# A state-space layer and a mixture-of-experts transformer layer on one core: PSUM banks and products regrouped in the second phase

## The reference, cut to what matters

```python
h = rmsnorm(x, ln1_w)
q, k, v = split(h @ wqkv.T)                # 16 query heads, 4 key/value heads, 8 features each, rope on q and k
scores = q @ k.T * scale                   # causal
attn = softmax(scores) @ v
x = x + attn @ wo.T
h = rmsnorm(x, ln2_w)
logits = h @ gate_w.T                      # 8 experts
topw, topi = top_k(softmax(logits), 2)     # two experts a token, weights normalised
for e in range(8):
    g = silu(h @ w1[e].T) * (h @ w3[e].T)  # 256 wide
    out = out + (g @ w2[e].T) * wfull[:, e:e + 1]
return x + out
```

## Time and profile before

| | us |
|---|---|
| median of 3 runs | 2104.83 (2100.11 to 2111.2) |
| the profiled execution | 2109.42 |
| its span | 2107.6 |
| mean granted clock of PE | 0.802 of full speed |

### The profile page before, as it was taken

How to read it: one execution, slowest core, us unless ns; L and a number is a source line. 1 busy time by engine, 2 the same in 40 slices (tenths; PEclk the granted TensorE clock), 3 DMA queues, 4 the chain that set the end, 5 groups by cost and what they waited for, 6 DMA issues and landing times.

```text
span 2107.6 us, 29882 instructions
## 1 busy us (share of the span) xinstructions
PE 1465.6 (70%) x8536; PEld 1038.4 (49%) x8536; DVE 1600.7 (76%) x2570; ACT 1138.5 (54%) x1901; POOL 1377.4 (65%) x1224
## 2 busy tenths in 40 slices
PE   3767676676666677666527777788787887888663
PEld 1544454454445455444413444565656565656553
DVE  3999999999999999999614656566767666765443
ACT  4655565655556565556112775656565656565410
POOL 1776777777777777677542775648676767767633
PEclk8887777887777888777555988889888888888877
DMA  4210212220121212022021012424252433442453
GB/s 157 86 66 32 85 80 101 80 100 10 74 97 80 101 80 79 22 81 96 5 60 34 28 43 73 125 75 131 88 151 91 141 97 106 129 128 84 136 175 104
DMA packets 113890, 185.00 MB, mean 88 GB/s; under 512 B 9856, under 2 KB 86656, under 8 KB 109440
## 3 DMA queue, kind: packets, MB, share of 16 engines
q1 hardware_dynamic: 109664, 175.14, 24.5%
q0 software_dynamic: 4096, 8.40, 1.4%
HBM read 153.03 MB, written 25.89 MB: 85 GB/s over the span
## 4 chain that ended last, share of the span: by engine, by line
PE 18%; DVE 11%; POOL 7%; issue 6%; DMA 5%; ACT 2%; SPq 1%; another core or an unknown queue 0%; POOLq 0%; DVEq 0%; ACTq 0%
PE og L1306 3%; DVE mx L1678 3%; POOL pp L2033 3%; PE ms L1252 2%; POOL xs_scratch L2042 2%; DMA xg<-xs_scratch 2%; PE pbk L1375 2%; PE po L1385 2%; PE scores L1287 1%; PE ms L1250 1%; DVE rec L1707 1%; PE pa L1368 1%; DMA xs_scratch<-h2n,posi 1%; DVE h L1640 1%; PE m L1347 1%
## 5 line engine op out<-in xcount | busy, mean ns | idle before, releaser
L731 POOL TENSOR_TENSOR hc<-hb,cb 128x512 f32<-128x512 f32 x512 | 654.5, 1297 | 248.2 <-DVE hb L610 218.4
L610 DVE TENSOR_TENSOR_SCAN hb<-da,dbu 128x512 f32<-128x512 f32 x512 | 598.9, 1200 | 5.6 <-DVE stats L635 4.0
L499 ACT ACTIVATE da<-dt,a_neg 128x512 f32<-128x512 f32 x512 | 351.9, 717 | 353.8 <-DVE hb L610 302.6
L2033 POOL TENSOR_TENSOR pp<-pt,pp 128x512 f16<-128x512 f32 x320 | 377.6, 1184 | 230.1 <-ACT pt L1534 225.4
L1678 DVE TENSOR_REDUCE mx<-ms 128x1 f32<-128x384 f32 (+3 forms) x352 | 224.8, 639 | 298.4 <-PE ms L1252 296.4
L331 PE MATMUL yp<-ident,hc 128*128 128x128 f32 x2048 | 358.6, 317 | 66.0 <-POOL hc L731 65.6
L331 PEld LDWEIGHTS yp<-ident,hc 128*128 128x128 f32 x2048 | 297.8, 165 | 175.4 <-POOL hc L731 94.2
L1533 ACT ACTIVATE pp<-scores,lift 128x512 f16<-128x512 f32 x320 | 219.0, 684 | 205.7 <-PE scores L1287 203.2
L603 DVE TENSOR_TENSOR dbu<-dtu,bp 128x512 f32<-128x512 f32 x512 | 323.2, 675 | 3.0 <-PE bp L319 1.6
L319 PE MATMUL bp<-st,sel 96*128 96x512 bf16 x256 | 116.5, 456 | 155.3 <-DVE dbu L603 152.9
L1534 ACT ACTIVATE pt<-scores,lift 128x512 f32<-128x512 f32 x320 | 218.8, 684 | 0.0
(11 more groups left out here) (194 smaller groups left out, 2436.0 us busy)
## 6 DMA issues: line engine op xcount, KB each, us to landing
cb<-c_scratch SPq DMA_DIRECT2D x16, 3072.0 KB, 11.9
wt<-ffn_w_e SPq DMA_DIRECT2D x120, 384.0 KB, 3.8
cb<-c_scratch SPq DMA_DIRECT2D x16, 1024.0 KB, 4.6
q<-q_scratch SPq DMA_DIRECT2D x96, 96.0 KB
xg<-xs_scratch SPq DMA_DIRECT2D x8, 960.0 KB, 5.7
ys_scratch<-ysb SPq DMA_DIRECT2D x24, 256.0 KB, 2.3
q_scratch<-qp SPq DMA_DIRECT2D x24, 128.0 KB
k<-k_scratch SPq DMA_DIRECT2D x32, 72.0 KB
```

The costliest lines, as they stand in the source:

```text
L499: nc.scalar.activation(da[:, s % NDA, :], dt[:, d, h, :], ACT.Exp, scale=a_neg[:, d, h, n:n + 1]).then_inc(da_done, 1)
L610: nc.vector.tensor_tensor_scan(hb[:, s % NHB, :], da[:, s % NDA, :], dbu[:, s % 2, :], 0.0, ALU.mult, ALU.add).then_inc(scan_done, 1)
L731: nc.gpsimd.tensor_tensor(hc[:, s % NHC, :], hb[:, s % NHB, :], cb[:, d, s // 2, :], ALU.mult).then_inc(hc_done, 1)
L2033: nc.gpsimd.tensor_tensor(pp[:, (ST_TILES * b + t) % NPR, 1, 0:width], pt[:, (ST_TILES * b + t) % NPR, 0:width], pp[:, (ST_TILES * b + t) ...
```

## The change

- The bank `pbk` is gone; `ms` has two banks, used in turn, and `pe_max(t)` waits for the reduction before the last one. The experts' rows, gate and up products all use `pa`: `pe_a` of f = 0 waits for `xt`, `pe_bm` for `ga` of its own half, `pe_a` of f = 1 for `g` of the first half.
- The down products have slots of their own (`down_at`: f = 0 nine and f = 1 thirteen slots behind 10q), and the copy out of `po` comes in slot 10q + 14 (`out_at`). For q = 3 these are slots 39, 3 and 4.
- For the masks of several heads there is one product with the mask repeated, over a strided output, in `pe_max` and `pe_st`.
- The count is in bf16 (`prefix` converted once by POOL, `chosen` written as bf16) and has five products instead of eleven: those of earlier blocks and the sum are one product a block, with `chosen` repeated. It moves from slot 25 to 27.
- `dve_gate`'s steps get slots by the table `GATE_AT` (20 to 32); the three steps of `wsum` and `wn` move from the end (24 to 26) to 12 to 14, so all later steps have numbers higher by three. The scatters move to slots 31 to 38.

```diff
+GATE_AT = (20, 20, 21, 21, 21, 22, 22, 23, 23, 24, 25, 25, 26, 26, 26, 28, 28, 28, 29, 29, 29, 30, 30, 31, 31, 32, 32)
...
+def down_at(b, t):
+
+    for q in range(NG):
+        for f, at in ((0, 10 * q + 9), (1, 10 * q + 13)):
+            found = b - 2 - at // ST_TILES
+            if t == at % ST_TILES and valid(found):
+                return found, q, f
+    return None
...
+def out_at(b, t):
+
+    for q in range(NG):
+        at = 10 * q + 14
+        found = b - 2 - at // ST_TILES
+        if t == at % ST_TILES and valid(found):
+            return found, q
+    return None
...
-        chosen = sb("chosen", [P, TC, NE])
+        chosen = sb("chosen", [P, TC, NE], BF16)
...
-        pbk = pb("pbk", [P, SEQ])
         po = pb("po", [P, SEQ])
         m0 = pb("m0", [P, SEQ])
-        ms = pb("ms", [P, SEQ])
+        ms = pb("ms", [P, 2, SEQ])
...
-            pe.wait_ge(max_done, count(max_done, b, t))
+            pe.wait_ge(max_done, count(max_done, b, t - 1))
             width = (c + 1) * P
+            heads = ms[:, t % 2, 0:n * width].rearrange("p (n k) -> p n k", n=n)
+            nc.tensor.matmul(heads[:, :, c * P:width], identb[:, :], mask[:, 0, :].unsqueeze(1).to_broadcast([P, n, P]),
+                             start=True, stop=False, skip_group_check=True)
             for i in range(n):
-                at = i * width
-                nc.tensor.matmul(ms[:, at + c * P:at + width], identb[:, :], mask[:, 0, :],
-                                 start=(i == 0), stop=False, skip_group_check=True)
-                last = nc.tensor.matmul(ms[:, at:at + width],
-                                        q9[0:PART_ROWS, h0_ + i, c * P:(c + 1) * P],
+                last = nc.tensor.matmul(heads[:, i, :], q9[0:PART_ROWS, h0_ + i, c * P:(c + 1) * P],
                                         k9[0:PART_ROWS, (h0_ + i) // 4, 0:width],
                                         start=False, stop=True, skip_group_check=True)
             last.then_inc(max_ready, 1)
...
-            for i, (h, kc, at) in enumerate(pieces(t)):
-                nc.tensor.matmul(sp_[:, t % 2, at:at + P], identb[:, :], mask[:, 1, :],
-                                 start=(i == 0), stop=False, skip_group_check=True)
+            ps = pieces(t)
+            blocks = sp_[:, t % 2, :].rearrange("p (n k) -> p n k", k=P)[:, 0:ps[-1][2] // P + 1:max(ps[-1][2] // P, 1)]
+            nc.tensor.matmul(blocks, identb[:, :], mask[:, 1, :].unsqueeze(1).to_broadcast([P, len(ps), P]),
+                             start=True, stop=False, skip_group_check=True)
+            for h, kc, at in ps:
...
-            for c in range(TC - 1):
-                for later in range(c + 1, TC):
-                    nc.tensor.matmul(m0[:, later * NE:(later + 1) * NE], prefix[:, 1, :], chosen[:, c, :],
-                                     start=False, stop=False, skip_group_check=True)
             for c in range(TC):
-                last = nc.tensor.matmul(m0[:, TC * NE:(TC + 1) * NE], prefix[:, 1, :], chosen[:, c, :],
+                later = m0[:, (c + 1) * NE:(TC + 1) * NE].rearrange("p (n e) -> p n e", e=NE)
+                last = nc.tensor.matmul(later, prefix[:, 1, :], chosen[:, c, :].unsqueeze(1).to_broadcast([P, TC - c, NE]),
                                         start=False, stop=(c == TC - 1), skip_group_check=True)
             last.then_inc(cnt_ready, 1)
...
-                last = nc.tensor.transpose(pbk[:, i * P:(i + 1) * P], xg[:, j, :], ident[:, :])
+                last = nc.tensor.transpose(pa[:, i * P:(i + 1) * P], xg[:, j, :], ident[:, :])
             last.then_inc(xg_ready, 1)
 
         def pe_a(pe, b, q, f):
-            n = NF * q + f
             if f == 0:
                 pe.wait_ge(w_loaded[q], count(w_loaded[q], b, 16 * len(tiles(q))))
-            pe.wait_ge(ga_done, count(ga_done, b, n))
-            pe.wait_ge(xt_done, count(xt_done, b, q + 1))
+                pe.wait_ge(xt_done, count(xt_done, b, q + 1))
+            else:
+                pe.wait_ge(g_done, count(g_done, b, NF * q + 1))
             for i, j in enumerate(tiles(q)):
                 last = nc.tensor.matmul(pa[:, i * P:(i + 1) * P], wt[:, j % NWT, f * P:(f + 1) * P], xt[:, j * P:(j + 1) * P],
                                         start=True, stop=True)
             last.then_inc(a_ready, 1)
 
         def pe_bm(pe, b, q, f):
-            pe.wait_ge(g_done, count(g_done, b, NF * q + f))
+            pe.wait_ge(ga_done, count(ga_done, b, NF * q + f + 1))
             for i, j in enumerate(tiles(q)):
-                last = nc.tensor.matmul(pbk[:, i * P:(i + 1) * P], wt[:, j % NWT, FF + f * P:FF + (f + 1) * P],
+                last = nc.tensor.matmul(pa[:, i * P:(i + 1) * P], wt[:, j % NWT, FF + f * P:FF + (f + 1) * P],
                                         xt[:, j * P:(j + 1) * P], start=True, stop=True)
             last.then_inc(b_ready, 1)
...
             q, j = k // 5, k % 5
             if j == 0:
-                if q > 0:
-                    pe_down(pe, b, q - 1, 1)
-                elif valid(b - 1):
-                    pe_down(pe, b - 1, NG - 1, 1)
                 pe_xg(pe, b, q)
             if j == 1:
                 pe_a(pe, b, q, 0)
@@ -1403,7 +1418,6 @@
                 pe_a(pe, b, q, 1)
             if j == 4:
                 pe_bm(pe, b, q, 1)
-                pe_down(pe, b, q, 0)
...
-                    if t == 25:
+                    if t == 27:
+                        if post == 0:
+                            pe.wait_ge(casts, 3)
                         pe_count(pe, post)
...
                 if step := moe_at(b, t):
                     pe_moe(pe, *step)
-                elif t == 2 and valid(end):
-                    pe_down(pe, end, NG - 1, 1)
+                if step := down_at(b, t):
+                    pe_down(pe, *step)
...
-                elif t == 2 and valid(end):
-                    act_y(act, end, NG - 1)
+                if step := out_at(b, t):
+                    act_y(act, *step)
...
-                    if t == 20:
-                        dve_gate(dve, post, 0)
-                    if 21 <= t <= 33:
-                        dve_gate(dve, post, 2 * (t - 21) + 1)
-                        dve_gate(dve, post, 2 * (t - 21) + 2)
+                    for k in range(GATE_STEPS):
+                        if t == GATE_AT[k]:
+                            dve_gate(dve, post, k)
...
-                    if 30 <= t < 30 + TC * TOP:
-                        pool_scatter(pool, post, t - 30)
+                    if 31 <= t < 31 + TC * TOP:
+                        pool_scatter(pool, post, t - 31)
...
+                if b == 1:
+                    pool.wait_ge(rest_loaded, n_rest)
+                    nc.gpsimd.tensor_copy(prefix[:, :, :], prefix32[:, :, :]).then_inc(casts, 1)
```

More of the change, by code:

```diff
@@ L865, in ffn_phase @@
         tri = sb("tri", [P, NE, NE])
-        prefix = sb("prefix", [P, 2, P])
+        prefix32 = sb("prefix32", [P, 2, P])
+        prefix = sb("prefix", [P, 2, P], BF16)
         pick = sb("pick", [P, TOP])
@@ L1037, in ffn_phase @@
                          (mask32, "mask"))
-        rest_weights = ((wo, "wo"), (gate, "gate"), (tri, "tri"), (prefix, "prefix"), (pick, "pick"), (full, "full"),
+        rest_weights = ((wo, "wo"), (gate, "gate"), (tri, "tri"), (prefix32, "prefix"), (pick, "pick"), (full, "full"),
                         (tile_no, "tile_no"))
@@ L1123, in sp_w @@
         def sp_w(sp, b, q):
-            chosen_by = count.in_register(sp, gate_step, b, 24)
+            chosen_by = count.in_register(sp, gate_step, b, 27)
             used = count.in_register(sp, down_done, b, NF * (q - 1))
@@ L1216, in pe_ht @@
             if valid(b - 3):
-                pe.wait_ge(gate_step, count(gate_step, b - 3, 17))
+                pe.wait_ge(gate_step, count(gate_step, b - 3, 20))
             for c in range(TC):
@@ L1263, in pe_nm @@
                 else:
-                    pe.wait_ge(gate_step, count(gate_step, b - 2, 17))
+                    pe.wait_ge(gate_step, count(gate_step, b - 2, 20))
             elif valid(b - 1):
@@ L1317, in pe_wo @@
             else:
-                pe.wait_ge(gate_step, count(gate_step, b - 1, 17))
+                pe.wait_ge(gate_step, count(gate_step, b - 1, 20))
             for c in range(TC):
@@ L1768, in dve_gate @@
             if k == 12:
+                i = v.tensor_tensor(wsum[:, 0, :], wk_[:, :, 0], wk_[:, :, 1], ALU.add)
+            if k == 13:
+                i = v.reciprocal(wsum[:, 1, :], wsum[:, 0, :])
+            if k == 14:
+                i = v.tensor_tensor(wn[:, :, :], wk_[:, :, :], wsum[:, 1, :].unsqueeze(2).to_broadcast([P, TC, TOP]),
+                                    ALU.mult)
+            if k == 15:
                 dve.wait_ge(cnt_ready, count(cnt_ready, b, 1))
@@ L1826, in dve_xt @@
             n = len(tiles(q)) * P
-            nc.vector.tensor_scalar(xt[:, q * SEQ:q * SEQ + n], pbk[:, 0:n], lnw[:, 1:2], None,
```

(3 more changed lines are left out.)

39 lines of the change are left out of this document (13 added, 26 removed).

## The result

The changed kernel takes 2053.73 us (median of 4 runs, 2052.77 to 2056.9) against 2104.58 us (4 runs); the ratio is 0.9761, with a 95% interval of 0.9737 to 0.9784. It is faster by 51 us; the forecast was 2043 us, 62 less. The profiled execution has a span of 2052.8 us, 54.8 less than before.

The account below looks back on a forecast made before the run. PE, in order and waiting for others, was taken as nearest to the bound. Steady periods -41, batch 6 -8, batches 0, 1 and 7 -4, -9, -4, start -10, tail +14: total -62, giving 2043 us; range 2025 to 2062.

Parts of the forecast that it names:

- The count: Count moved from slot 25 to 27: five bf16 products replace 22 fp32 records, so 4.2 us go.
- Slot 25's wait: PE's 3.14 us wait for `chosen` goes; with the count, `bm` of slot 26 begins 6.3 us earlier.
- the DVE region: From `bm` of slot 26 to slot 30, DVE has 9 us of work where 13.3 passed; 1.8 us gained.
- The second bank: PE may run one maximum ahead, cutting waits for `mx`: 1.6 plus 1.6 us a period, 10 at the start.
- The shared bank: Rows, gate and up in `pa`: waits hidden while DVE is at most one slot behind; 1 us lost a period.
- `y` leaves two slots later, which the gather in slot 6 covers: Down products only change slots; the later `y` costs nothing, with 5 us for a 2.3 us store.
- POOL's queue: Slots 31 to 39: scatters, splits and rope parts, ending in `kf`, finish 1 us earlier a period.
- Tail: Experts alone, shared bank in the open: 16 us over eight groups, 3 for low clock, 5 given back; +14.
- (1): Less gain: DVE stays in lockstep, PE waits every even slot; steady period gives 3.5 us, about 2081 us; chance 0.15.
- (2): More gain: low-clock stretches and nearly all `mx` waits go; 7 us more a period, about 1995 us; chance 0.15.
- (3): Slower: `bm` waits in the open every even slot of steady periods; 16 us a period, about 2127 us; chance 0.06.
- (4): PE's granted clock falls from 0.89 to 0.80, costing 10 us in each of six periods; about 2103 us; chance 0.04.

Follow-up runs that it names:

- The routing part alone: Changed kernel with banks and down products as before; count, routing and scatter places and merged masks as changed: 2066.7 us, ratio 0.9823 to the kernel before.

## Why the prediction came out as it did

The time, 2053.7, lies in the forecast's own range (2025 to 2062), and the sign of every part was right. That the total came so near is partly luck, as the table shows. But by the marks that it set itself its steady period was wrong: 108.6 us where it was not to stay above 107, the new waits for `ga` were at their limit of 5 a period (19.8 in four), and the gap of slot 25 moved, to slot 26 instead of 27, with two thirds of its size. Point by point:

- **The count** (-4.2 us in slot 25): right. No wait for `chosen`, 0.2 us of records, and 3.6 us of price when the fp32 form is put back.
- **Slot 25's wait** (the other part of -6.3) **and the DVE region** (-1.8): the step failed. The prediction let `ga` follow "3.01 us of `h`", a duration read from the earlier trace rows, where three POOL instructions lay beside it. It came out at 4.29, with 1.13 for a copy of 0.16: POOL now runs splits and output steps for 5.6 us without a pause, before for 4.5. Taking POOL's output steps away from there brought a part of `h` back to 440 ns; what made POOL denser was not tried by itself. `bm` started 7.8 us behind the exponential of slot 24; before it was 13.9, so 6.1 us were gained on that product, about the 6.3 forecast, but what is left of the gap stands in slot 26 (8.7 us). Slots 25 and 26 together went from 14.9 to 9.9: 5.0 us of 6.3, and of this slot 23 gave back 3.1 (3.3 to 6.4), where ranking steps are now crowded and stretched in the same way. Behind it the DVE region gave its share: slots 29 and 30 are 2.9 us shorter. The routing part alone brought 5.3 us a period instead of 8.1.
- **The second bank** (-3.2 a period, -10 at the start): right in place, too small in size. PE's waits for `mx` went from 42.6 to 7.1 us in four periods and 60 us hang on it in all, beside a shared expert bank. At the start 14.2 us went instead of 10, and came back with one bank. The prediction had put most of the waits down to times when "DVE itself is full", and so counted a third of them.
- **The shared bank** (+1.0 a period, +14 in the tail): the mechanism was right, and the size too small by more than half; with the down products' new places it costs 47 us. The step that failed was its condition: DVE is more than one slot behind in slot 26 of batches 3 to 5, so the wait is in the open once in each of them, for 5.5 us. In the tail a group takes 12.9 to 15.2 us (the first 19.7) instead of the 10.4 in series; the prediction had started from the shortest group of before (8.4 us), while the others in the same tail took 9.9 to 17.3.
- **"`y` leaves two slots later, which the gather in slot 6 covers"**: wrong, and it cost 22 us. It looked only at who reads `y`, not at what stands behind it in SyncE's queue. For a copy that is moved, the DMA behind it counts too.
- **POOL's queue** (-1.0) **and the load of `xg`** (+1.1): the wait for `xg` grew by 1.5 us a period (6.2 to 12.0 in four), as forecast. The gain is not to be seen: ACT's wait for `kf` grew from 17.3 to 22.3, and slots 30 to 39 take 29.8 us in batches 3 to 5, as before, though slot 30 alone is 1.1 us shorter.
- **The masks** (nothing): right. The 1.2 us a period and 10 us in all by the rule of the Trainium skill ("TensorE: Matmul & The Clock Gate", Back-to-back issue gap), an estimate from its 81 ns, did not come.
- **Tail** (+14): 21.6. The shared bank was 10 of it and the late `y` 7; with both taken out it is 141.0 us, and the last 4 us are not explained. POOL's gather waits 51.8 us for the stores of `y` in this tail, against 32.6 in the routing part alone, whose tail is 134.5.

Of the rivals, (1) named what happened in batches 3 to 5 (they gave 3.2 us each, as it said, 3.5), though by other waits than its own: those for `mx` did go, and DVE held PE up for `ga` mainly in one slot of the period and not in every even one. (2) had it right that the waits for `mx` go nearly whole, but only batch 2 and the early parts gained beyond the forecast. (3), the shared bank in the open, is true once a period and not eight times. (4) did not come: the granted clock rose from 0.89 to 0.91 in the steady period.

## What to carry to other kernels

When a PSUM bank is moved from one user to another, price both sides as a wait: here it was 60 us won and 47 lost, and the difference would have been missed by looking at either. A duration read beside a certain load on POOL does not hold when the change makes POOL denser: read what ran beside it, and how far its instructions differ. The four parts of `h` took 3.0 us in each of three periods before, which looks safe, but the single parts took 334 to 1298 ns. And a copy that is moved later takes its store along, with all that stands behind that store in the queue, so put the last store of a stage ahead of the next stage's. The move of POOL's output steps failed by the same rule.

## What the runs showed of the hardware

- A part of `h` (128x128, fp32, one per-partition scalar pair, on DVE) took 333 ns where POOL was idle and up to 1299 where POOL ran without a gap; a copy of 8 columns took 0.16 or 1.13 us. In the dense stretch shown above each ended within 0.1 us of the end of a POOL instruction.
- A `tensor_tensor` of 128x256 in the ranking (the step `gtm`) took 424 ns before and 1302 to 1303 in three periods after, in the crowded slots, with the one ahead of it 415 in the same periods. So the kind of instruction alone doesn't say what is stretched: the step `ended` (128x120) took 1166 ns before, and 282 after.
- Repeating a 128-column block in the moving operand, or writing over a strided output, cost no measurable time (2053.7 against 2054.7 us; 0.11 us for 256 columns at the full clock).
- Cycling two banks for the maxima did not lower the granted clock (0.91 in the steady period, 0.89 before).
